# Attention scores on four 32-column strips of the array, keys in four pieces

## The reference

```python
q = rope(rmsnorm(x @ Wq.T)); k = rope(rmsnorm(x @ Wk.T)); v = x @ Wv.T   # 32 query heads, 8 key heads, 128 each
k_all = concat([k_cache[block_table], k])        # 16 pages of 32 keys, and the 32 new ones: 544 keys
v_all = concat([v_cache[block_table], v])
scores = einsum('bqhd,bkhd->bhqk', q, k_all) * SCALE   # 4 query heads share one key head
scores = where(valid, scores, -1e30)
probs = softmax(scores)
o = einsum('bhqk,bkhd->bqhd', probs, v_all)
x = x + o @ Wo.T
# then three layers x = x + base(x) + lora(x)
```

## Time and profile before

| | |
|---|---|
| time, median of 2 runs | 2340.1 us (2339.66 to 2340.54) |
| profiled execution, its span from first to last instruction | 2339.1 us |
| what the median of the runs has beyond that span | 1.0 us |
| PE busy over the span | 2311.7 us (99%) |
| DVE, ACT, POOL busy | 1488.0, 1356.3, 508.3 us |
| granted TensorE clock, mean of the span | 0.995 |
| attention on PE, first and last score product start | 550.0 to 1766.7 us |

### The profile page before, as it was taken

One profiled execution on the slowest core, in us unless ns is written; L12 is line 12 of the kernel. 1 busy time (PEld: TensorE's weight loads), 2 busy tenths in 40 slices (PEclk: granted clock), 3 DMA queues, 4 the chain that ended last, 5 costly groups with the idle time before them and its releaser, 6 DMA issues.

```text
span 2339.1 us, 48442 instructions
## 1 busy us (share of the span) xinstructions
PE 2311.7 (99%) x14320; PEld 1999.4 (85%) x14320; DVE 1488.0 (64%) x4154; ACT 1356.3 (58%) x4300; POOL 508.3 (22%) x538
## 2 busy tenths in 40 slices
PE   8999999998999999999999999999999999999998
PEld 7887777777999999999999999999998888888886
DVE  5899999983666666666666666666665344334433
ACT  4878888874666666666666666666665222222221
POOL 5211221211223333332222222222223011011101
PEclk9999999999999999999999999999999999999998
DMA  5344444448999999898998999999885333333331
GB/s 207 92 126 114 112 127 116 111 113 283 342 344 293 294 290 289 292 290 289 294 289 283 295 295 292 289 290 295 292 295 178 99 101 106 93 100 108 94 101 43
DMA packets 400360, 488.63 MB, mean 209 GB/s; under 512 B 63136, under 2 KB 334752, under 8 KB 397216
## 3 DMA queue, kind: packets, MB, share of 16 engines
q1 hardware_dynamic: 363296, 351.93, 49.3%
q0 software_dynamic: 36864, 134.23, 17.2%
HBM read 397.89 MB, written 88.08 MB: 208 GB/s over the span
## 4 chain that ended last, share of the span: by engine, by line
PE 77%; DVE 15%; issue 4%; SPq 1%; DMA 1%; DVEq 1%; ACT 0%; ACTq 0%
PE s_bank L1010 20%; PE o_bank L1022 19%; PE pt L1057 10%; DVE q_t L668 5%; PE proj L1509 5%; PE proj L1511 5%; PE proj L1510 5%; DVE part_s L659 5%; DVE q_t L684 5%; PE o_bank L1038 2%; PE slim L1540 1%; PE wide L1556 1%; PE wide L1551 1%; PE wide L1552 1%; PE turn L1530 1%
## 5 line engine op out<-in xcount | busy, mean ns | idle before, releaser
L977 DVE CUSTOM_DVE_ANT_0 probs<-s_bank,mask 128x544 f32<-128x544 f32 x512 | 371.1, 725 | 426.5 <-PE s_bank L1010 425.0
L931 ACT ACTIVATE probs<-probs,neg_max 128x544 f32<-128x544 f32 x512 | 383.9, 750 | 405.1 <-DVE neg_max L977 405.1
L1010 PE MATMUL s_bank<-k_t,q_t 128*128 128x288 f32 (+1 forms) x2048 | 558.3, 396 | 6.6 <-DMA q_t<-q_spill 4.4
L1022 PEld LDWEIGHTS o_bank<-p_t,v_c 128*128 128x128 f32 x4096 | 527.9, 192 | 28.8
L1022 PE MATMUL o_bank<-p_t,v_c 128*128 128x128 f32 x4096 | 540.1, 275 | 0.0
L1010 PEld LDWEIGHTS s_bank<-k_t,q_t 128*128 128x128 f32 x2048 | 351.2, 192 | 63.4 <-DMA q_t<-q_spill 4.8
L138 POOL DMA_INDIRECT v_c<-in_v_rows,v_row x256 | 255.2, 997 | 300.9 <-PE o_bank L1022 260.3
L1057 PE MATMUL pt<-ident,probs 128*128 128x128 f32 x2048 | 311.3, 275 | 0.0
L737 PE MATMUL acc<-w_hi,x_hi 128*128 128x512 f32 x764 | 304.6, 399 | 0.1
L903 ACT ACTIVATE p_t<-pt 128x512 f32<-128x512 f32 x512 | 295.9, 578 | 10.3 <-PE pt L1057 1.2
L738 PE MATMUL acc<-w_lo,x_hi 128*128 128x512 f32 x764 | 299.8, 392 | 0.0
(11 more groups left out here) (152 smaller groups left out, 3299.8 us busy)
## 6 DMA issues: line engine op xcount, KB each, us to landing
k_t<-in_k_pages SPq DMA_DIRECT2D x1024, 128.0 KB
q_spill<-wo_early SPq DMA_DIRECT2D x512, 64.0 KB, 1.8
q_t<-q_spill SPq DMA_DIRECT2D x64, 512.0 KB
o_spill<-o_t SPq DMA_DIRECT2D x64, 512.0 KB, 5.3
raw<-o_spill SPq DMA_DIRECT2D x64, 512.0 KB, 3.5
k_t<-in_w_qkv SPq DMA_DIRECT2D x11, 1024.0 KB, 5.7
v_spill<-wo_early SPq DMA_DIRECT2D x8, 1024.0 KB, 6.6
k_spill<-wo_early SPq DMA_DIRECT2D x128, 64.0 KB, 1.8
```

What stands on the lines that cost most here:

```text
L931: nc.scalar.activation(probs[:, j % SLOTS_P], probs[:, j % SLOTS_P], ACT.Exp, scale=-1.0, bias=neg_max[:, j % 2:j % 2 + 1], accum_out=row_ ...
L977: nc.vector.tensor_tensor_reduce(out=probs[:, j % SLOTS_P], in0=s_run, in1=mask[:, par], scale=-SCALE, scalar=3.0e38, op0=ALU.add, op1=ALU ...
L1010: last = pe.matmul(s_bank[:, columns].rearrange("p (s t) -> p s t", t=PSIZE), q_t[:, par, g], k_t[:, par, slots, g], start=True, stop=True)
L1022: last = pe.matmul(o_of(n), v_c[:, par, c, g * HD:(g + 1) * HD], p_t[:, i, c], start=g < QUAD and c == 0, stop=False)
```

## The change

The product of all 128 query rows with a piece of the keys becomes four products of 32 query rows each. Each has the 32 columns of its query rows as weights, in a 32-column strip of the array of its own, and writes the 32 PSUM partitions that belong to it. The keys are cut in four pieces of 5, 4, 4 and 4 slots (160, 128, 128 and 128 columns). For each piece the four strips come one after the other. So a unit has 16 score products, 32 passes, where it had 2 products, 4 passes. The semaphore `scored` is still incremented once, by the last.

```diff
+    PARTS = ((0, 5), (5, 4), (CUT, 4), (CUT + 4, 4))
...
-                for columns, slots in ((slice(BANK - CUT * PSIZE, BANK), slice(0, CUT)),
-                                       (slice(BANK, BANK - CUT * PSIZE + KEYS), slice(CUT, NPP + 1))):
-                    last = pe.matmul(s_bank[:, columns].rearrange("p (s t) -> p s t", t=PSIZE), q_t[:, par, g],
-                                     k_t[:, par, slots, g], start=True, stop=True)
+                for first, n in PARTS:
+                    columns = slice(BANK + (first - CUT) * PSIZE, BANK + (first + n - CUT) * PSIZE)
+                    for a in range(QUAD):
+                        rows = slice(a * S, (a + 1) * S)
+                        last = pe.matmul(s_bank[rows, columns].rearrange("p (s t) -> p s t", t=PSIZE), q_t[:, par, g, rows],
+                                         k_t[:, par, first:first + n, g], start=True, stop=True)
                 last.then_inc(scored, 1)
```

## The result

The changed kernel takes 2509.1 us (median of 2 runs, 2508.93 to 2509.32) against 2340.1 us: ratio 1.0719, 95% interval 1.0688 to 1.075. It is slower by 169 us. Forecast were 2537 us, and 2490 to 2600 for the likeliest case.

The account below looks back on a forecast made before the run. PE was taken to bound the kernel (99% busy, chain never leaving it in attention). Streaming, drains, stagger and exposed loads summed to 0.385 us a unit, times 512 is 197 us: 2537 us, range 2490 to 3030.

Parts of the forecast that it names:

- the likeliest case: Attention's score step: the four strips overlap fully, 2537 us, 2490 to 2600 us; chance 62%.
- step on streaming: Score products: eight passes a strip, four strips at the same time, 0.94 in place of 0.92 us, +0.02 us a unit.
- two drains: PE going over to strips before the scores and going back after them: +0.09 us of drain each, per unit.
- exposed load on the way back: Full 128-column load after the strips: +0.11 us before the weighted values, 0.05 before a transpose in one unit of four.
- the term of the first strip load: First 32-column load on going over to strips, exposed: +0.07 us a unit, between 0.03 and 0.11.
- the width that was added for the drains: Widening of the likeliest case's 2517 to 2558 us for drains half as long or half as long again: 46 us.
- The term for issue: 64 instead of 8 PE instructions a unit in the score step: no cost, but no reserve shown.
- signs: Expected in the changed profile: score link 1.15 to 1.2 us, next link +0.2, grouped passes, two gaps, longer DVE idle time.
- part overlap: Rival: strips hold each other up or each load is exposed, scores about +0.94 us a unit, 3018 or 3028 us; chance 18%.
- double rate on strips: Rival: a strip takes a column at twice the rate, 2307 us, or 2120 to 2290 with shorter drains; part of 15%.
- idle time of VectorE: VectorE's (DVE's) idle time before L977, waiting for scores, grows by about 0.385 us a unit.

## Why the prediction was right

Its step on streaming held, which was the one on which all hung: the four column strips overlap fully. 32 passes take 1.06 us with a drain, a first load and the stagger in it, and the time grows only when the order of the strips keeps them apart. The row strips of L1038 were the right row for it: the same groups of four, the same distance.

The two drains were read off L1038 at 0.09 us each and came out so: 0.20 us from the last transpose to the first strip load, and again from the last strip pass to the full-width load. The exposed load on the way back held as well, about 0.10 us before the values and 0.05 before a transpose (with the drain, +0.20 and +0.15 in the links behind).

Mis-sized was the term of the first strip load. It was put at 0.07 us, the middle between four loads together (0.03) and four in a row (0.11); it measured 0.03, the lower end: the second set of passes starts 0.16 us after the first. That is 0.04 us a unit, 20 of the 28 us between forecast and result. Another 5 us or so are the streaming term, +0.02 in the forecast; in the timeline a strip's eight passes fill 0.93 us, +0.01. The last 3 us are within the rounding of the other terms. Because two terms erred the same way, the result lies 8 us below 2517, the lower end of the sum itself, and in the range by the width that was added for the drains. That width was worked out wrongly at its lower end: 2517 less 46 is 2471, not 2490. The term for issue (none) was right.

The trace does not agree with the rule of the Trainium skill, "TensorE: Matmul & The Clock Gate", Part 3, that a weight load overlaps with a running matmul only where the row group differs: in the changed kernel the loads of a strip started at 1301.29 and 1301.43 with passes of all strips, hence of the same row group, under way. Had each of the 32 loads been exposed, the score step would have been about 1 us longer (the forecast's 32 x 0.03).

One of the signs did not fit the forecast's own sum: it names 1.15 to 1.2 us for the score link, while the terms that fall into that link (0.92 + 0.02 + 0.09 + 0.07 + 0.02) make 1.12; it measured 1.06. Of the other signs these came as named: the link behind longer by 0.20, the groups 0.136 and 0.11 us apart, the gap of 0.2 us on either side.

The rivals: part overlap is real, but as a matter of order, at 2960 and 3296 us in the kernels that hand a strip 6 or 8 passes in a row. A double rate on strips did not show: sets of 160 columns are 0.14 us apart, sets of 128 are 0.11. The idle time of VectorE grew by 0.33 us a unit, where 0.385 was forecast, the same mis-sized term.

## What to carry to other kernels

Cutting the output rows of a product into column strips saves nothing when each strip still has to stream every column: the stream is as long as before, and what is left is the price of the mode. On this kernel one visit to strips between full-width products costs about 0.3 us, however much or little is done in it (0.29 with one product, 0.33 with sixteen), so it has to save more than that. Visits that can stand side by side should: values on strips right behind scores on strips cost no second visit (-0.07 us), with a transpose between them they did (+0.27). If strips are used, deal the products out across them, at most four passes to a strip in a row, and two rather than four (2509 against 2527 us).

## What the hardware showed beyond what was expected

- A strip holds three passes back behind the one it streams, and the other strips go on meanwhile. Up to four passes in a row overlap (2509 us with two, 2527 us with four), with six the next strip starts 0.30 us later (2960 us), with eight 0.52 us (3296 us).
- Going from full width to strips and back showed a drain of 0.09 us each way, and a first load that nothing covers: 0.03 us into the strips, 0.10 us before the values, 0.05 us before a transpose.
- Four loads of 32 columns on four column strips together take 0.03 us; a load of 128 columns takes 0.11.
- Each further full-width pass that splits the same columns costs about 5 ns, 10 us for 2048 of them.
- On strips the four products of the weighted values took 0.87 us against 0.89 at full width: the passes themselves were a little faster there (0.109 us apart against 0.112).
